# Graph network head: P of all blocks ahead of Q, visit tables beside P, sum tables zeroed from GpSimd's queue

## What is computed

```python
hi, hj = x[src], x[dst]                       # e[0] = src, e[1] = dst
msg = silu(concat(hi, hj, d2) @ mW1 + mb1)
msg = silu(layer_norm(msg, g, b) @ mW2 + mb2)
agg = segment_sum(msg, src)                   # 6250 rows of 256
x1  = layernorm(x + (x + silu(concat(x, agg) @ uW1 + ub1) @ uW2 + ub2))
mean = segment_sum(x1[src], dst) / counts
out = layernorm(x1 + relu(mean @ W.T + b))
```

## Time and profile before

| | us |
|---|---|
| median of 3 runs | 4269.81 (4268.96 to 4271.36) |
| the profiled execution | 4270.8 |
| its span, first to last instruction | 4269.1 |
| up to the first matmul of picks | 19.9 |
| picks, up to the first transpose of x | 19.9 to 46.8 |
| P and Q of 50 blocks, with their last VectorE instruction | 46.8 to 179.7 |
| lead of the message loop, from the first gather to the first silu | 180.7 to 272.9 |
| from there to the first indirect add to a sum table | 272.9 to 296.6 |

### The profile page before, as it was taken

The page is one execution under the profiler, slowest core; times in us unless marked ns, Lnnn a source line. Parts: engine busy times, 40 slices in busy tenths (PEclk is TensorE's granted clock), DMA queues, the critical chain, the costliest instruction groups (busy, mean ns, idle before and its releaser), DMA issues.

```text
span 4269.1 us, 77955 instructions
## 1 busy us (share of the span) xinstructions
PE 3217.0 (75%) x15999; PEld 2355.7 (55%) x16000; DVE 2687.8 (63%) x12003; ACT 1508.6 (35%) x2737; POOL 2993.0 (70%) x2621
## 2 busy tenths in 40 slices
PE   7667777777777777777777777879577777777776
PEld 3246656666656565666666666658444444444445
DVE  6356666666666666666666666767755554445457
ACT  2224545555554555455554455553200000000005
POOL 0258888888888888888888888761177777777762
PEclk9768999989999989899989999999888888888888
DMA  4665555555555555555555555575433333333333
GB/s 149 191 196 94 93 96 92 95 93 93 95 93 95 93 93 96 93 95 93 95 94 93 95 93 94 82 140 164 142 105 104 105 104 104 104 105 104 104 85 115
DMA packets 336082, 455.19 MB, mean 107 GB/s; under 512 B 53568, under 2 KB 282524, under 8 KB 335772
## 3 DMA queue, kind: packets, MB, share of 16 engines
q0 software_dynamic: 199680, 327.32, 40.9%
q1 hardware_dynamic: 116844, 105.48, 8.5%
q10 hardware_dynamic: 19248, 19.66, 1.3%
HBM read 296.41 MB, written 155.62 MB: 106 GB/s over the span
## 4 chain that ended last, share of the span: by engine, by line
POOL 30%; PE 25%; issue 19%; DMA 16%; DVE 6%; ACT 1%; DVEq 1%; SPq 1%; ACTq 0%; POOLq 0%
POOL sum L574 17%; POOL arena L563 12%; PE ps L855 9%; DMA arena<-x_tab,esrc 9%; DMA sum<-arena,sidx 5%; PE ps L859 3%; PE ps L758 3%; PE ps L809 2%; PE ps L721 2%; PE ps L745 1%; POOL arena L604 1%; DVE arena L1380 1%; PE ps L827 1%; DMA arena<-loc_tab 1%; PE ps L731 1%
## 5 line engine op out<-in xcount | busy, mean ns | idle before, releaser
L574 POOL DMA_INDIRECT sum<-arena,sidx x832 | 1317.6, 1584 | 291.5 <-issue 243.9
L563 POOL DMA_INDIRECT arena<-p_tab,esrc x832 | 812.1, 976 | 447.7 <-issue 416.4
L604 POOL DMA_INDIRECT arena<-x_tab,esrc x832 | 794.0, 954 | 305.9 <-issue 143.8
L855 PE MATMUL ps<-arena 128*125 x1760 | 666.9, 467 | 348.7 <-DMA arena<-x_tab,esrc 299.2
L758 PE MATMUL ps<-w,arena 128*128 128x256 f32 x3328 | 839.3, 385 | 3.9 <-ACT arena L985 3.9
L855 PEld LDWEIGHTS ps<-arena 128*125 128x125 f32 x1760 | 381.3, 227 | 613.2 <-issue 530.1
L1348 DVE TENSOR_TENSOR arena<-ps,arena 128x256 f32 x880 | 373.6, 425 | 549.1 <-DMA arena<-p_tab,esrc 335.2
L1549 DVE TENSOR_TENSOR arena<-ps,arena 125x257 f32 x880 | 374.6, 426 | 508.4 <-PE ps L855 481.5
L758 PEld LDWEIGHTS ps<-w,arena 128*128 128x128 f32 x3328 | 572.9, 192 | 122.1 <-issue 5.0
L731 PE MATMUL ps<-ident,arena 128*128 128x128 f32 x1664 | 271.7, 316 | 459.7 <-DVE arena L1380 459.3
L721 PE MATMUL ps<-arena 128*128 128x256 f32 x1664 | 525.3, 473 | 2.4 <-ACT arena L975 2.2
(11 more groups left out here) (192 smaller groups left out, 3998.3 us busy)
## 6 DMA issues: line engine op xcount, KB each, us to landing
arena<-loc_tab SPq DMA_DIRECT2D x220, 125.0 KB
arena<-sum SPq DMA_DIRECT2D x200, 128.0 KB, 2.2
sum<-scr ACTq DMA_DIRECT2D x3, 6400.0 KB, 57.7
arena<-p_tab,esrc POOLq DMA_INDIRECT x832
sum<-arena,sidx POOLq DMA_INDIRECT x832, 3.9
arena<-x_tab,esrc POOLq DMA_INDIRECT x832, 2.7
sum<-scr SPq DMA_DIRECT2D x1, 6400.0 KB, 22.1
arena<-x_tab SPq DMA_DIRECT2D x50, 128.0 KB, 2.0
```

Source lines behind the costliest of these rows:

```text
L563: pool.indirect_dma_start(out=ring0[:, tile % RING, :], out_offset=None, in_=p_tab[:, :], in_offset=bass.IndirectOffsetOnAxis(ap=esrc[:, t ...
L574: pool.indirect_dma_start(out=sums[u][:, :], in_=tot[:, par, u, :], in_offset=None, out_offset=bass.IndirectOffsetOnAxis(ap=sidx[:, par, u ...
L604: pool.indirect_dma_start(out=ring[:, tile % LATER_RING, 0:D], out_offset=None, in_=x1_tab[:, :], in_offset=bass.IndirectOffsetOnAxis(ap=e ...
L855: nc.tensor.matmul(ps[0:NB, u, 0:CW], same1[:, par, u, :], ring[:, bass.ds(at[u], 1), :].rearrange("p a c -> p (a c)"), start=True, stop=T ...
```

## The change

Picks, P and Q are put in another order:

- **P first, Q behind.** The 50 blocks run twice. A first pass, straight behind the ranges of the tiles, transposes x, makes P alone (matmuls of 256 columns) and stores it. The transposes of all blocks stay in SBUF (`xt`, in the upper part of `big`). A second pass makes Q from them (`q_step`). GpSimd's first gather no longer waits for Q, only TensorE's start of the message loop does.
- **Picks and visit tables within P.** The 7 chunks stand on VectorE behind blocks 0 to 6 and on TensorE behind blocks 3 to 9; the 22 instructions stand two behind each block from 11 on. Up to block 19 P has a single bank for transposes and a single one for products, since the picks hold six of the eight; from block 20 on it has two of each.
- **x by fives, P by twos.** SP loads x in 10 groups of 5 blocks into two slots and stores P in 25 pairs into two slots (two DMAs each, 112 and 13 partitions).
- **Zeros from GpSimd.** All four tables are zeroed from GpSimd's queue ahead of everything else that it issues, each in 5 DMAs of 640 rows of 2 KB. SP and ScalarE issue none.
- **The d2 row in three parts.** `weight_rows` writes blocks 0 to 15 at block 40 of P, 16 to 32 after 25 blocks of Q and 33 to 49 after all of Q, because `xt` lies there until then. TensorE waits for all three ahead of the message loop.

The diff, cut:

```diff
+        PICKS_AT, ESRC_AT, WTR_AT, WIDE_AT, PLACES_AT = 3, 12, 15, 20, 40
+        def column_bank(q):
+            return PK if q < WIDE_AT else PZ + q % 2
+        def product_bank(q):
+            return PK + 1 if q < WIDE_AT else PM + q % 2
+        def free_before(q):
+            return q if q < WIDE_AT else max(q - 1, 0) if q >= WIDE_AT + 2 else 0
...
         def zero_sums(eng, table):
+            for i in range(ZPIECES):
+                n = rows_ // ZPIECES
+                eng.dma_start(whole[:, i * n:(i + 1) * n, :], zeros[:, :].unsqueeze(1).to_broadcast([P, n, ZW]))\
+                    .then_inc(s_tables, 16)
...
+            for i in range(BLOCKS // PAIR):
+                if PAIR * i % XGROUP < PAIR and 2 <= PAIR * i // XGROUP + 1 < BLOCKS // XGROUP:
+                    load_x(PAIR * i // XGROUP + 1)
+                if PAIR * i == PLACES_AT:
+                    store_places()
+                    sp.wait_ge(s_wpart, 5)
+                    weight_rows(0)
+                sp.wait_ge(s_prow, PAIR * (i + 1))
...
             pool.wait_ge(s_constc, 8)
+            pool.wait_ge(s_zeroed, 1)
+            for t in sums:
+                zero_sums(pool, t)
...
-            pool.wait_ge(s_q3, BLOCKS)
-            pool.wait_ge(s_wrow, 16)
+            pool.wait_ge(s_slots, 9)
...
-            steps(pe, BLOCKS, 1, pq_step, by=XSLOTS, slots=XSLOTS, first=12)
+            for q in range(BLOCKS + 1):
+                p_step(q)
+            def q_step(q, par):
+                if later(q, 2):
+                    pe.wait_ge(s_qr, q - 1)
+                else:
+                    pe.wait_ge(s_prow, BLOCKS - 1 + q)
+                for h in range(H):
+                    last = nc.tensor.matmul(ps[0:NB, PM + par, 0:D], xt[:, q, h, 0:NB], w1[:, H + h, :],
+                                            start=h == 0, stop=h == H - 1)
+                last.then_inc(s_qmm, 1)
...
-            for t in sums[1:TABLES]:
-                zero_sums(ac, t)
```

More of the change, by code:

```diff
@@ L387, in _, with load_x @@
                         .then_inc(s_weights, 16)
-            def zero_tables():
-                sp.wait_ge(s_zeroed, 1)
-                for t in (p_tab, x1_tab):
-                    sp.dma_start(t[N:ROWS, :], zeros[0:NB, :]).then_inc(s_padrows, 16)
-                for t in sums[0:1]:
-                    zero_sums(sp, t)
+            def load_x(g):
+                if g >= 2:
+                    sp.wait_ge(s_xt, XGROUP * (g - 1))
+                rows_ = x[g * XGROUP * NB:(g + 1) * XGROUP * NB, :].rearrange("(j p) d -> p j d", p=NB)
+                for a, z in SPLIT:
+                    sp.dma_start(pxin[a:z, g % 2, :, :], rows_[a:z]).then_inc(s_xload[g % 2], 16)
+            for g in range(2):
+                load_x(g)
+            sp.wait_ge(s_zeroed, 1)
+            for t in (p_tab, x1_tab):
+                sp.dma_start(t[N:ROWS, :], zeros[0:NB, 0:D]).then_inc(s_padrows, 16)
             with sp.If(tiles_down(sp) > 0):
@@ L652, in sum_picks, with chunk @@
                 return last
-            for c in range(CHUNKS):
+            def chunk(c):
                 pe.wait_ge(s_pick, 2 * (c + 1))
@@ L664, in _ @@
                 last.then_inc(s_picked, 1)
-            for c in range(CHUNKS):
-                last = nc.tensor.transpose(ps[:, PK + c // 4, c % 4 * P:(c % 4 + 1) * P], ends[:, 0, c, :], ident[:, :])
-            last.then_inc(s_esrct, 1)
             def by_visit(rows_, bank):
@@ L698, in pq_step @@
                                                 start=h == 0, stop=h == H - 1)
-                    last.then_inc(s_pqmm, 1)
-            steps(pe, BLOCKS, 1, pq_step, by=XSLOTS, slots=XSLOTS, first=12)
+                    last.then_inc(s_pmm, 1)
+                if PICKS_AT <= q < PICKS_AT + CHUNKS:
+                    chunk(q - PICKS_AT)
+                if q == ESRC_AT:
+                    pe.wait_ge(s_blk, 1)
+                    for c in range(CHUNKS):
+                        last = nc.tensor.transpose(ps[:, PM + c // 4, c % 4 * P:(c % 4 + 1) * P], ends[:, 0, c, :],
+                                                   ident[:, :])
+                    last.then_inc(s_esrct, 1)
+                    pe.wait_ge(s_visit, 2)
+                    by_visit(vloc[:, :], PP)
@@ L702, in _ @@
+            for q in range(BLOCKS):
+                q_step(q, q % 2)
             s = e[0]
@@ L1196, in edge_parts, with pick_chunk @@
                 nc.vector.tensor_tensor(wparts[:, 2], wleft[:, :, :], wparts[:, 1], ALU.subtract).then_inc(s_epart, 1)
-            for c in range(CHUNKS):
+            def pick_chunk(c):
                 if c >= 2:
@@ L1289, in _, with p_step @@
             visits_ = visit_tables()
-            def pq_step(q, par):
+            TAKE_AT = PICKS_AT + CHUNKS
+            def p_step(q):
+                dve.wait_ge(s_pmm, q + 1)
+                pair, slot = q // PAIR, q // PAIR % 2
+                if pair >= 2:
+                    dve.wait_ge(s_pst[slot], pair // 2 * 32)
+                nc.vector.tensor_tensor(prow[:, slot, q % PAIR, :], ps[0:NB, product_bank(q), 0:D], b1b[0:NB, :], ALU.add).then_inc(s_prow, 1)
+                if q < CHUNKS:
+                    pick_chunk(q)
+                elif q < TAKE_AT:
+                    next(weights_, None)
+                    next(weights_, None)
+                elif q == TAKE_AT:
+                    take_picks()
+                else:
+                    for _ in range(2):
+                        if next(visits_, None) is None:
+                            next(weights_, None)
@@ L1292, in pq_step, with q_step @@
+            for q in range(BLOCKS):
+                p_step(q)
+            assert next(visits_, None) is None and next(weights_, None) is None
+            def q_step(q, par):
                 if live(q, BLOCKS):
-                    dve.wait_ge(s_pqmm, q + 1)
+                    dve.wait_ge(s_q1, q + 1)
                     if later(q, 2):
-                        dve.wait_ge(s_pst[par], half_count(q - 2) * 32)
                         dve.wait_ge(s_q3, q - 1)
-                    nc.vector.tensor_tensor(prow[:, par, :], ps[0:NB, PM + par, 0:D], b1b[0:NB, :], ALU.add)\
-                        .then_inc(s_prow, 1)
```

188 lines of the change are left out of this document (83 added, 105 removed).

## The result

The changed kernel takes 4286.02 us in the median (4283.07 to 4291.17, 7 runs), the kernel before beside it 4271.36 (4268.57 to 4279.12). The ratio is 1.0027, with a 95% interval of 1.0018 to 1.0037. The forecast was 4249. Two profiled executions are compared here: 4283.1 us (span 4281.3) now, 4270.8 (4269.1) before. The whole difference is there when the first add to a sum is issued: at 310.47 us now, at 296.58 before.

A forecast was written before the change was run, and what follows sets the result against it. The head's sequence up to the first silu was taken as the bound: start of the message loop at 189 us plus a lead of 62 gives 251, 20.6 earlier, so 4270.8 becomes 4250.2 and the median 4249; range 4234 to 4270.

The forecast's parts named there:

- first silu: ScalarE's preparation of the message loop's first silu: forecast at 251 us against 271.6, 20.6 us earlier, moving the time equally.
- the lead: Stretch from TensorE's start of the message loop (first expansion) to the first silu: 62 us against 90.8, bounds 59 and 81.
- Steps 2 and 3: P's blocks 0 to 9 with picks, to 59 us; then visit tables on VectorE's path, 26 us, to 85 at block 22.
- the places would be fast again: Loads of places in the lead: at most 4.76 us; the rival that they stay at 7 us had chance 0.12.
- Step 1: Start of P: 17.7 us plus 1.5 for weights competing with GpSimd's zeros (bounds 0 and 4), so 19.
- Steps 2 to 4: All of P after its start at 19 us: to 59, then 85 at block 22, ending at 132 to 133.
- the flood: Rival: zeros slow all of P through waits for stores; zeros until 150 us would give 4288; chance 0.10.
- Step 4: P's last 28 blocks: 5 at 2.9 us amid zeros until 100, 23 at 1.4; P ends at 132 to 133.
- My own sign of being wrong: Wrong if VectorE waits long for P's stores past 100 us, expansions stay 5.9 us apart, or message loop's pace differs.
- Step 6: The d2 row: 17 pieces after the last Q, 4 us, 2 hidden beside VectorE's last steps; TensorE starts at 189.
- the front would cost 8 us: Everything before the message loop: TensorE may start it at 189 us, 8 later than before; bounds 177 and 203.
- The rival on VectorE and GpSimd's port: VectorE's masks, casts and scalings in P, 15 us, hold up GpSimd's zeros to 115; start moves 8, 4257; chance 0.10.

The follow-up runs named there:

- e14: Changed kernel with three x slots, five store slots, 6 zero pieces beside picks and 14 beside Q, d2 row in four parts: 4241.0 us, ratio 0.9920.
- e6: Changed kernel, but GpSimd waits for the weights and two groups of x before its heap of zeros: 4279.8 us, ratio 1.0027.
- e15: Changed kernel with three slots for x and five for stores of P, zeros still at the very start: 4247.4 us, ratio 0.9939.
- e4: Changed kernel with three slots for x instead of two, each group loaded one group earlier: 4265.8 us, ratio 0.9981.
- e16: Changed kernel with five slots for stores of P, still two for x: 4274.0 us, ratio 1.0002.
- e17: e14 with 10 pieces of zeros beside the picks and 10 beside Q instead of 6 and 14: 4241.8 us, ratio 0.9922.
- e10: Changed kernel with its move of the zeros undone (SP and ScalarE issue them), new order kept: 4286.2 us, ratio 1.0042.
- e3: Kernel before, with only the zeros moved: all in 20 pieces from GpSimd's queue at its start: 4274.5 us, ratio 1.0003.
- e7: Changed kernel with three x slots, GpSimd waiting for weights and two groups of x before its heap of zeros: 4264.8 us, ratio 0.9990.
- e8: Changed kernel with three x slots and the 20 zero pieces paced, each behind a block of P: 4262.5 us, ratio 0.9984.
- e13: e8 with five slots for the stores of P: 4253.7 us, ratio 0.9951.

## Why the prediction was wrong

**The sum.** The first silu came 35.9 us later than forecast. By the sum's own terms that is 18.2 for the start of P, 13.7 from there to block 22, 4.6 for the blocks behind it and 3.8 for the d2 row, less 2.7 for Q and 1.7 for the lead. The runs show that these terms aren't separate: the start turns out to be worth little by itself.

**Right.** That everything hangs on the first silu: its shift is 15.3 us, the medians differ by 14.7. The length of the lead (60.3 against 62). My 62 lay between two limits, 59 by GpSimd and 66 by the places at 4.76 us a load, and I expected steps of 5 us a quad, GpSimd's. The places load in 3.2 to 4.6 us, which by the same formula (4.8 us and the load, for two quads) is 59 as well. The chain goes through them, in steps of 4.2 us a quad. That both limits come out equal is luck. Q: 51.3 us for 50 blocks against 54. Steps 2 and 3, the work of VectorE: where P starts at 19 us and waits for no store (e14, six pieces of zeros beside the picks), block 10 comes at 58.0 and block 22 at 83.9, against 59 and 85. That the places would be fast again, not 7 us.

**Step 1, start of P, mis-sized.** I took 1.5 us for the contention of the weights with the zeros, bounds 0 and 4. The weights landed 15.2 us later than before, and the first group of x held the start up for another 3, so 37.2 instead of 19. The bound came from a gather that GpSimd issued 7 us after ScalarE's zeros; here the whole heap is in the queues by 24.7 us, and the small loads are issued among and behind it. A nearer row stood in the trace of before: SP's load of x straight behind its own table of zeros held SP's queue for 17 us.

```profile
21.79 17.12 SPq L405 DMA_DIRECT2D arena<-in_x_dram  x2
```

The rule of the Trainium skill named in the prediction (DMA: Bandwidth & Descriptors, "Issuing engines are not separate DMA queues") says that DMAs run on the same engines whichever engine issues them, and the trace agrees: the zeros of GpSimd's queue keep the weights and x of SP's waiting, at a busy share of 1.04. It puts no price on that wait. But e6 shows that mending this step alone is worth 1.5 us at P's end: the earlier blocks met the same zeros.

**Steps 2 to 4, the pace of P: what failed.** Up to block 22 I had 66 us from the first transpose; it took 79.7 (37.2 to 116.9). The blocks behind it I had at 48, the first five of them amid zeros, and they took 53 (to 169.5), though amid no zeros at all; without waits they take 28.5 (e15, e14). Two terms were wrong.

- *The latency amid zeros.* I let a store land in 5 us, at most 7.6, and counted no wait for a store or for x before block 22. The chain shows 14.4 us for x and 10.7 for a store there, and 17.5 in e4. By the formula (0.85 + landing) / 2 that would be 5.8 to 9.2 us a block and not 2.9, if every pair waited. Only four waits for a store stand in the trace (14.9 us), beside those for x, and blocks 0 to 12 took 4.4 us each (40.7 to 93.6) where e15 takes 3.4. That was in part the mechanism of my last rival, the flood, which gave 4288 and had 0.10. I had tied it to a slow drain of the zeros, until 150 us. They had landed by 94, before my 100, and held P up all the same. That its number is near the measured one is in part luck.
- *Loads of x left out.* The sum had no term for them. Two slots of five blocks and a load that SP issues behind its waits for stores expose 5 us per group when blocks take 1.1 us: 9.1 us for five, 1.8 a block, against my 1.4. Before, four single slots at 2.03 us a block had hidden it. Stores matter here too, though the zeros are gone: one wait of 8.7 us stands before block 44. From block 22 to 49 it takes 52.6 us in the changed kernel, 44.5 with five slots for stores (e16), 41.2 with three for x (e4) and 28.5 with both (e15), 1.06 a block. Step 4 had neither wait, and that its 1.4 a block was more than 1.06 hid part of the error. My own sign of being wrong, long waits for stores past 100 us, named only that one wait of 8.7; six waits for x stood beside it.

**Step 6, the d2 row.** 5.8 us exposed instead of 2: 4.9 from issue to landing for 17 pieces, and no VectorE work beside it. By the pieces (12.3 us for 50) I had 4, and hid half of it behind steps that were already done. Splitting it finer (e14, e17) brought nothing that shows: 8.5 and 6.1 us for 6 blocks, with zeros still about.

**The claim that the front would cost 8 us.** It cost 45. The lead's gain of 30 was real, and the front gave it back with 15 more. Neither half of the change gains alone (e10, e3): in each the zeros still stand beside something that waits for small transfers.

**The rival on VectorE and GpSimd's port** falls by its size. In e7 GpSimd issues its 20 pieces from 21.2 us on, beside VectorE's masks and casts (7.0 of 10 us busy from 20 to 30, 5.0 from 30 to 40), at 0.93 us each; at the start of the changed kernel, with VectorE busy for 4.5 of the 18 us, it is 0.91. Neither is near the 15 us of delay that the rival took:

```profile
21.24 18.61 POOL L381 DMA_DIRECT2D sum<-scr  x20 [15.14 <-DMA arena<-in_x_dram]
```

Single pieces do show something. Most take 0.87 us. In e7 a mask or a cast begins during six of them: four of these take 1.02 to 1.18 us, and beside a fifth the cast takes 0.95 us instead of 0.62. The changed kernel has one such piece:

```profile
10.12 1.50 POOL L377 DMA_DIRECT2D sum<-scr  x1
10.13 1.09 DVE L1116 CAST arena<-arena 128x1792 f32<-128x1792 int32 x1 [9.99 <-DMA arena<-in_edge_weight_dram]
```

So the rule of the Trainium skill (SBUF — State Buffer, "Who interferes with whom") agrees with the trace in kind: a piece can wait for an operation of VectorE. In e7 that comes to 1 us over all 20 pieces, and GpSimd's queue doesn't starve.

**TensorE's clock** was granted at 0.83 over 30 to 90 us and 0.84 over 100 to 170, so the four matmuls of a block behind a wait took 1.72 us instead of 0.87. In e15, with the waits gone, the same blocks run at 1.00 from 90 us on: the low clock came with the waits, and made each a little dearer.

## What to carry over

Here the price of a transfer of many megabytes was not set by its bandwidth but by what was issued beside it. So look for a stretch in which no engine waits for small loads or stores (here the picks and Q). Where there is none, count the slots by the latency beside the transfer (here 14 to 17 us), not by that of idle DMA engines. When a stage is split and becomes twice as fast per step, recompute every double buffer of it, loads and stores, since the waits lie one behind the other and removing one shows only part of the gain (12 and 17 us alone, 39 together). Mending a delay at the start of a chain that later waits for the same resource was worth little (1.5 to 2.4 us of 13 to 18).

## What was not expected of the hardware

- Twenty DMAs of 1.25 MB are issued by GpSimd in 18.3 us, and land 36.7 us after issue in the median; behind such a heap SP's issue of two 0.5 KB vectors takes 2.57 us instead of 0.91, and four DMAs of x hold its queue for 12.6.
- Under a full load (busy share 1.02 to 1.04, 380 to 398 GB/s in the windows above) a store of a pair of blocks takes up to 17.5 us (e4) and a load of five blocks of x up to 20.9 (the first of e15), against about 5 once the zeros have gone.
- Dealing the zeros out in single pieces behind P's blocks didn't lower that latency: a store took 14.3 us in e8 (64.67), and a load of x 19.1 in e13.
- A piece of zeros whose issue meets the start of a cast or a mask on VectorE can take 1.0 to 1.5 us instead of 0.87, but over the 20 pieces of e7 that adds up to 1 us.
